# Two chains of handed-over transposes in place of one, and the near maximum between two decay multiplications, in an attention block on one core

## The reference

```python
def _L0_attn_ref(x, W_attn, W_proj):
    ...
    att = jnp.einsum('bhqd,bhkd->bhqk', q, k) * (1.0 / math.sqrt(hd))
    causal = jnp.tril(jnp.ones((T, T), dtype=bool))
    att = jnp.where(causal, att, -jnp.inf)
    att = jax.nn.softmax(att, axis=-1)
    att = att * decay_weight_matrix(T)
    y = jnp.einsum('bhqk,bhkd->bhqd', att, v)
    y = y.transpose(0, 2, 1, 3).reshape(B, T, HEAD_QKV)
    return y @ W_proj
...
h = _layernorm(x, axis=-1) * (1 + ca) + sa
x = x + ga * _L0_attn_ref(h, L0_attn_W_attn, L0_attn_W_proj)
h = _layernorm(x, axis=-1) * (1 + cb) + sb
x = x + gb * _L0_ffn_ref(h, ...)
```

## Time and profile before

| what | us |
|---|---|
| time, median of 3 runs (range) | 1622.48 (1616.28 to 1624.26) |
| the profiled execution's own time | 1620.14 |
| its span | 1618.3 |
| busy in the span: TensorE | 1301.4 |
| busy in the span: ScalarE | 1325.7 |
| busy in the span: VectorE | 974.1 |
| attention, first to last exponential | 203.4 to 1520 |

### The profile page before, as it was taken

How to read it: one execution, slowest core, us unless ns; L and a number is a source line. 1 busy time by engine, 2 the same in 40 slices (tenths; PEclk the granted TensorE clock), 3 DMA queues, 4 the chain that set the end, 5 groups by cost and what they waited for, 6 DMA issues and landing times. The chain is left out here.

```text
span 1618.3 us, 27960 instructions
## 1 busy us (share of the span) xinstructions
PE 1301.4 (80%) x11067; PEld 751.6 (46%) x11067; DVE 974.1 (60%) x1562; ACT 1325.7 (82%) x2677; POOL 52.4 (3%) x28
## 2 busy tenths in 40 slices
PE   7863188888888888888888888888888888777698
PEld 5532044444444444444444444444444444333387
DVE  5631166666666666666666666666666655544366
ACT  3433099999999999999999999999999999999532
POOL 0222000000000000000000000000000000000022
PEclk9987599999999999999999999999999999999689
DMA  4999930101010101010101010101010101000144
GB/s 165 189 232 212 147 51 1 33 2 34 1 34 1 33 1 34 1 33 2 34 1 34 1 34 1 34 1 23 9 20 11 23 9 23 8 7 1 35 152 135
DMA packets 111722, 72.95 MB, mean 45 GB/s; under 512 B 56396, under 2 KB 110947, under 8 KB 111587
## 3 DMA queue, kind: packets, MB, share of 16 engines
q1 hardware_dynamic: 111586, 71.13, 20.7%
HBM read 45.93 MB, written 25.17 MB: 44 GB/s over the span
## 5 line engine op out<-in xcount | busy, mean ns | idle before, releaser
L888 ACT ACTIVATE fast_s_ps<-fast_s_ps,fast_negmax 128x1024 f32<-128x1024 f32 (+4 forms) x768 | 789.5, 1029 | 42.4 <-PE fast_s_ps L792 40.8
L792 PE MATMUL fast_s_ps<-k_stack,fast_q_stack 96*128 96x512 bf16 (+3 forms) x2448 | 630.2, 356 | 139.4 <-ACT fast_probs L888 67.9
L918 DVE TENSOR_TENSOR fast_probsT<-fast_t_ps,fast_dec_c 128x640 f32<-128x640 f32 (+4 forms) x512 | 399.6, 780 | 216.7 <-PE fast_t_ps L812 205.7
L910 DVE TENSOR_REDUCE fast_negmax<-fast_s_ps 128x1 f32<-128x640 f32 (+4 forms) x512 | 400.1, 782 | 127.8 <-PE fast_s_ps L795 121.3
L888 ACT ACTIVATE fast_probs<-fast_s_ps,fast_negmax 128x640 f32<-128x640 f32 (+7 forms) x512 | 434.6, 849 | 51.0 <-DVE fast_negmax L910 43.7
L812 PE MATMUL fast_t_ps<-ident,fast_probs 128*128 128x128 f32 x2400 | 367.7, 282 | 102.9 <-DVE fast_yT_sb L924 50.9
L792 PEld LDWEIGHTS fast_s_ps<-k_stack,fast_q_stack 96*128 96x128 bf16 x2448 | 193.1, 98 | 400.0 <-ACT fast_probs L888 138.0
L812 PEld LDWEIGHTS fast_t_ps<-ident,fast_probs 128*128 128x128 f32 x2400 | 263.8, 141 | 201.3 <-DVE fast_yT_sb L924 85.7
L827 PE MATMUL fast_t_ps<-fast_probsT,fast_vals 128*16 128x128 f32 x4800 | 182.0, 277 | 3.9 <-DVE fast_probsT L918 2.2
L888 ACT ACTIVATION_READ_ACCUMULATOR fast_s_ps<-fast_s_ps,fast_negmax 128x1 f32 x768 | 164.2, 214 | 0.0
L827 PEld LDWEIGHTS fast_t_ps<-fast_probsT,fast_vals 128*16 128x16 f32 x4800 | 110.0, 96 | 77.1 <-issue 55.8
(11 more groups left out here) (104 smaller groups left out, 528.9 us busy)
## 6 DMA issues: line engine op xcount, KB each, us to landing
parts_d<-part SPq DMA_DIRECT2D x48, 256.0 KB, 12.4
k_stack<-parts_d SPq DMA_DIRECT2D x48, 256.0 KB, 9.6
fast_q_stack<-parts_d SPq DMA_DIRECT2D x192, 64.0 KB, 3.0
fast_vals<-v_d SPq DMA_DIRECT2D x36, 128.0 KB, 3.2
xs<-x_dram SPq DMA_DIRECT2D x8, 512.0 KB, 8.6
v_d<-w SPq DMA_DIRECT2D x8, 512.0 KB, 8.5
y_d<-fast_y_sb SPq DMA_DIRECT2D x32, 128.0 KB, 2.6
yy<-y_d SPq DMA_DIRECT2D x16, 256.0 KB, 2.7
```

The source lines that it names most:

```text
L792: last = nc.tensor.matmul(s_ps[:, n % SLOTS, o:o + w], q, k_stack[:, h, P * b0 + o:P * b0 + o + w], start=True, stop=not diag)
L888: nc.scalar.activation(dst, src, ACT.Exp, bias=negmax[:, p % 2, side, h:h + 1], scale=-1.0, accum_out=sums[:, p % 2, side, h, c:c + 1]).th ...
L910: nc.vector.tensor_reduce(out=negmax[:, p % 2, side, h:h + 1], in_=s_ps[:, n % SLOTS, max(0, cols - P * WIN):cols], axis=AX_X, op=ALU.min) ...
L918: nc.vector.tensor_tensor(probsT[:, turned(side, s), 0:nb, :], t_ps[:, 0:P * nb].rearrange("p (b q) -> p b q", q=P), dec_c[:, WIN - nb:WIN ...
```

## The change

`t_ps` gets two chains. The first bank belongs to the **head** of a unit, its first three blocks (`turn`, `decay`), and to `turn_back`. The second bank (`tail_ps`) belongs to the **tail** of a unit, its remaining one or two blocks (`turn_tail`, `decay_tail`, both new), and to the groups' values. Each chain has its own numbers and semaphores (`tail_no`, `tail_full`, `tail_free` for the second). A unit of up to three blocks has no tail.

- TensorE, near unit: the tail is turned right behind the head.
- TensorE, far unit: in a group step the head is turned ahead of part 1 of the values (before: all five blocks behind it), then come part 1, chunk 4 and only then the tail. In the other steps the tail is turned right behind the head.
- VectorE: `decay` is cut into a head and a tail. The tail of the last near unit comes behind the maximum of the near chunk of this step. The copy of a group comes between the two parts of the far unit.
- `values` waits until the tail chain is empty up to its own number, which takes in the tail of the near unit of the step before.

The diff, with the core of each place:

```diff
+            def has_tail(side, s):
+                return blocks(tile_of(s // NH, side)) > HEAD
+
+            def next_unit(side, s):
+                next_turn("unit", side, s)
+                if has_tail(side, s):
+                    next_tail("unit", side, s)
...
             for s in range(NSTEP):
                 if s > 0:
-                    next_turn("unit", NEAR, s - 1)
+                    next_unit(NEAR, s - 1)
                 if group_after(s):
-                    next_turn("group", *group_after(s))
+                    next_tail("group", *group_after(s))
                 if back_after(s):
                     next_turn("back", *back_after(s))
-                next_turn("unit", FAR, s)
+                next_unit(FAR, s)
...
+                tail_ps = t_ps[:, BANK:2 * BANK]
                 g_ps = t_ps[:, 2 * BANK - P:2 * BANK]
...
-                        for b in range(nb):
+                        for b in range(min(HEAD, nb)):
...
+                    def turn_tail(side, s):
+
+                        if not has_tail(side, s):
+                            return
+                        n = tail_no["unit", side, s]
+                        if n > 0:
+                            pe.wait_ge(tail_free, n)
...
+                        for b in range(HEAD, nb):
+                            lo = P * (b1 - b0 - nb + b)
+                            last = nc.tensor.transpose(tail_ps[:, P * (b - HEAD):P * (b - HEAD + 1)],
+                                                       probs[:, side, lo:lo + P], ident[:])
+                        last.then_inc(tail_full, 1)
+
                     def values(side, k, part):
 
-                        n = turn_no["group", side, k]
-                        pe.wait_ge(turn_free, n)
+                        pe.wait_ge(tail_free, tail_no["group", side, k])
...
                         if s > 0:
                             turn(NEAR, s - 1)
+                            turn_tail(NEAR, s - 1)
                         fill(s, 1)
                         fill(s, 2)
                         if group_after(s):
                             values(*group_after(s), 0)
                         fill(s, 3)
-                        if group_after(s):
-                            values(*group_after(s), 1)
                         if back_after(s):
                             side, done = back_after(s)
                             turn_back(done, side)
                         turn(FAR, s)
-                        fill(s, 4)
+                        if group_after(s):
+                            values(*group_after(s), 1)
+                            fill(s, 4)
+                            turn_tail(FAR, s)
+                        else:
+                            turn_tail(FAR, s)
+                            fill(s, 4)
...
-                                act.wait_ge(turn_full, turn_no["unit", side, s - 1] + 1)
+                                if has_tail(side, s - 1):
+                                    act.wait_ge(tail_full, tail_no["unit", side, s - 1] + 1)
+                                else:
+                                    act.wait_ge(turn_full, turn_no["unit", side, s - 1] + 1)
...
+                    def decay_tail(side, s):
+                        if not has_tail(side, s):
+                            return
+                        dve.wait_ge(tail_full, tail_no["unit", side, s] + 1)
+                        p, h = step_of(s)
+                        nb = blocks(tile_of(p, side))
+                        nc.vector.tensor_tensor(probsT[:, turned(side, s), HEAD:nb, :],
+                                                tail_ps[:, 0:P * (nb - HEAD)].rearrange("p (b q) -> p b q", q=P),
+                                                dec_c[:, WIN - nb + HEAD:WIN, :], ALU.mult).then_inc(tail_free, 1)
...
                         maximum(NEAR, s)
-                        if group_after(s):
-                            group_to_sb(*group_after(s))
+                        if s > 0:
+                            decay_tail(NEAR, s - 1)
...
                         decay(FAR, s)
+                        if group_after(s):
+                            group_to_sb(*group_after(s))
+                        decay_tail(FAR, s)
```

More of the change, by code:

```diff
@@ L666, in step_of, with next_tail @@
                 return s // NH, s % NH
-            turn_no = {}
+            HEAD = 3
+            turn_no, tail_no = {}, {}
             def next_turn(*job):
                 turn_no[job] = len(turn_no)
+            def next_tail(*job):
+                tail_no[job] = len(tail_no)
+            def has_tail(side, s):
[4 more added lines that the diff above has]
+                    next_tail("unit", side, s)
             def group_after(s):
@@ L688, in attention_fast @@
                 if s > 0:
-                    next_turn("unit", NEAR, s - 1)
+                    next_unit(NEAR, s - 1)
                 if group_after(s):
-                    next_turn("group", *group_after(s))
+                    next_tail("group", *group_after(s))
                 if back_after(s):
                     next_turn("back", *back_after(s))
-                next_turn("unit", FAR, s)
-            next_turn("unit", NEAR, NSTEP - 1)
+                next_unit(FAR, s)
+            next_unit(NEAR, NSTEP - 1)
             for side in (FAR, NEAR):
-                next_turn("group", side, NSTEP // HG - 1)
+                next_tail("group", side, NSTEP // HG - 1)
             for side in (FAR, NEAR):
@@ L709, in attention_fast @@
             turn_free = sem("fast_turn_free")
+            tail_full = sem("fast_tail_full")
+            tail_free = sem("fast_tail_free")
             y_stored = [sem(f"fast_y_stored{b}") for b in range(2)]
@@ L768, in _ @@
                             sp.wait_ge(s_full, PER * NH * p)
-                            sp.wait_ge(turn_full, turn_no["group", NEAR, NG4 * p - 1] + 1)
+                            sp.wait_ge(tail_full, tail_no["group", NEAR, NG4 * p - 1] + 1)
                             load(p + 1)
@@ L813, in turn @@
                         last.then_inc(turn_full, 1)
+                    def turn_tail(side, s):
[4 more added lines that the diff above has]
+                            pe.wait_ge(tail_free, n)
+                        p, _ = step_of(s)
+                        i = tile_of(p, side)
+                        b0, b1 = split(i)[0]
+                        nb = blocks(i)
+                        for b in range(HEAD, nb):
[3 more added lines that the diff above has]
+                        last.then_inc(tail_full, 1)
                     def values(side, k, part):
-                        n = turn_no["group", side, k]
-                        pe.wait_ge(turn_free, n)
+                        pe.wait_ge(tail_free, tail_no["group", side, k])
                         p, h = step_of(HG * k)
@@ L831, in values @@
                                 if b == nb - 1 and j == HG - 1:
-                                    last.then_inc(turn_full, 1)
+                                    last.then_inc(tail_full, 1)
                     def turn_back(p, side):
@@ L917, in decay @@
                         nb = blocks(tile_of(p, side))
-                        nc.vector.tensor_tensor(probsT[:, turned(side, s), 0:nb, :],
-                                                t_ps[:, 0:P * nb].rearrange("p (b q) -> p b q", q=P),
-                                                dec_c[:, WIN - nb:WIN, :], ALU.mult).then_inc(turn_free, 1)
+                        n = min(HEAD, nb)
+                        nc.vector.tensor_tensor(probsT[:, turned(side, s), 0:n, :],
+                                                t_ps[:, 0:P * n].rearrange("p (b q) -> p b q", q=P),
+                                                dec_c[:, WIN - nb:WIN - nb + n, :], ALU.mult).then_inc(turn_free, 1)
+                    def decay_tail(side, s):
[7 more added lines that the diff above has]
+                                                dec_c[:, WIN - nb + HEAD:WIN, :], ALU.mult).then_inc(tail_free, 1)
                     def group_to_sb(side, k):
-                        dve.wait_ge(turn_full, turn_no["group", side, k] + 1)
-                        nc.vector.tensor_copy(yT_sb[:, side, k % NG4, :], g_ps).then_inc(turn_free, 1)
+                        dve.wait_ge(tail_full, tail_no["group", side, k] + 1)
+                        nc.vector.tensor_copy(yT_sb[:, side, k % NG4, :], g_ps).then_inc(tail_free, 1)
                     def factors(p):
```

2 lines of the change are left out of this document (added).

## The result

The changed kernel takes 1720.97 us (median of 4 runs, 1718.82 to 1723.69), the kernel before 1622.26 us (median of 4, 1616.28 to 1624.26). The ratio is 1.0616, 95% interval 1.0584 to 1.0648. The profiled execution has a span of 1721.7 us, 103 us more than the one before.

A forecast was written before the change was run, and what follows sets the result against it. ScalarE was taken to set the pace, with group steps held by a chain through TensorE and VectorE; +0.96 us per usual group step, 83 + 6 + 5 - 6 = +88 us on 1620.1, gave 1708 us, range 1689 to 1737.

The forecast's parts named there:

- The new wait and its size: Group step: values wait for the near tail queued behind the near maximum, so part 0 starts 1.33 us later in pair 0.
- The end of the group step: From chunk 3 to the next exponential, the earlier far head shortens the chain from 3.97 to 3.60 us, gaining 0.37.
- The pairs: Sum over 126 group steps: 83 us for 86 usual ones, 6 pair 7, 5 pair 12, -6 pairs 13 to 15.
- my sum: Total of the pairs' terms, +88 us on the profiled 1620.1 us, with bounds of +69 and +117 us.
- The clock: Rival, 11%: TensorE falls to the lower clock in a quarter of 102 group steps, 33 us more, 1741 us.
- matmuls per us: Argument against the clock rival: pairs 0 to 12 would have 7.4, above pair 13 with 7.2, still at clock 1.00.
- The splits cost nothing in the plain steps: Splitting decays adds 140 ns per unit on VectorE, put at nothing in plain steps; rival, 8%: 0.14 us each, 1726 us.
- Absorbed: Rival, 5%: ScalarE's queued work covers the late values, only the end's gain counts, 47 us won, 1573 us.
- cancel: Rival, 4%: the end of a group step wins about 1.3 us, offsetting the late values, so 1620 us.

The follow-up runs named there:

- run 1: Changed kernel with VectorE's near tail decay moved ahead of the near maximum in every step: 1562.1 us, 0.9655 of the kernel before.
- run 2: Kernel before, one chain and whole decays, with only VectorE's near maximum moved ahead of the last near unit's decay: 1934.5 us in one run.
- run 4: Changed kernel with chunk 3 computed two extra times on TensorE ahead of part 0 of the values, where it waited: 1693.1 us, 1.0471 of the kernel before.
- run 5: Near tail first, plus the far tail turned behind the next step's chunk 0 and decayed behind its far maximum: 1575.4 us, 0.9755 of the kernel before.
- run 6: Changed kernel with the near tail's decay ahead of the near maximum in group steps only: 1568.0 us, 0.9696 of the kernel before.
- run 7: Early far maximum, near tail first in group steps only, and TensorE's near tail behind chunk 1 after a group step: 1551.5 us, 0.9582 of the kernel before.

## Why the prediction was right

**The new wait and its size.** Right, and within 0.03 us in pair 0. Worked out and measured, in us from the start of the group step: values 2.09 and 2.09, chunk 3 2.87 and 2.87, far head 3.31 and 3.32, copy 4.46 and 4.44, far tail 4.81 and 4.78, far maximum 5.62 and 5.60, next exponential 6.47 and 6.45. Values wait 103 times, where I had named 102; I had missed the first step of pair 13. ScalarE's waits in that step are a little shorter than forecast, 0.42 us for chunk 3 (0.5) and 0.94 for the far maximum (1.1). Outside the 21 long ones the group steps of pairs 4 to 7 take some 6.2 us, a little under the 6.3 to 6.6 that I had named. Runs 1 and 2 show that this one place in VectorE's order is the cause: moved back it turns the change into a gain, and put alone into the kernel before it costs more than the change.

**The end of the group step.** Right: a gain of 0.39 from chunk 3 on (3.97 to 3.58), 0.37 in the prediction. Run 1 has it on its own: 5.51 to 5.13.

**The pairs.** Somewhat too high. Run 4, in which the clock plays hardly a part, has a span of 1690.3 us, 72 us above the kernel before, where my sum was 88. The group steps of pairs 0 to 12 are 85 us longer in it than in the kernel before, where I had 94. In the usual group step the term was nearly right: 0.94 us in pair 0, 0.89 in pairs 4 to 6 (5.35 to 6.24), 0.77 in pair 7 (5.46 to 6.23). It was too large for the third and fifth step of each pair, which I had counted like the others: these took some 5.7 us already before and grow by only 0.59 us on average in pairs 1 to 6 and 8 to 11. For pair 12 it was too small, 0.94 us where I took 0.65. In pairs 13 to 15 the gain was too small: the group steps of these pairs sum to 126.2 us before and 117.6 after, 9 us where I took 6, and some 2.5 of the 9 are two steps that the kernel before ran at a lower clock (6.21 and 6.75 us, granted clock 0.73 and 0.71) and the changed one did not. The steps that are no group steps are 3 us shorter in run 4, where I took nothing.

**The clock.** This was a rival with 11%, for the case that a quarter of 102 group steps fall to the lower clock: 33 us. It happened in 21 of them and is worth 24 to 28 us by run 4, some 1.3 us for each, as worked out. So the time, 1721 us, is a mixture that the prediction did not name: its own mechanism at a somewhat smaller size, and most of a rival on top. That 1721 lies only 13 us above the forecast of 1708 is in part luck, since the chain came out some 16 us lower and the clock, at nothing in the sum, 24 to 28 us higher. My argument against the rival, matmuls per us averaged over pairs, did not tell: the average hides single waits of 1.25 us, and it was behind such a wait, after a stretch with TensorE busy 0.50 of 1.70 us, that the granted clock fell. The Trainium skill, TensorE: Matmul & The Clock Gate, Part 1, says that idleness lowers TensorE's clock and work restores it; the granted clock of 0.50 behind the wait and run 4 agree.

**The splits cost nothing in the plain steps.** Right: the usual one takes 4.72 us in the changed kernel, as before. There are 464 splits, not 458. VectorE is busy 1007.5 us instead of 974.1, 0.07 us per split and not 0.14. An instruction queued behind another starts some 0.08 us before that one's end, as the prediction read for the far maximum, and busy time counts such an overlap once; that would account for the difference.

**The rivals.** Absorbed and cancel did not come about; run 1 shows how little was missing for the first: the tail fits into 0.64 us of VectorE's idle time ahead of the near maximum.

## What to carry to other kernels

On an engine that works in order, look at what a short operation stands behind and at who waits for it. A tail of 0.41 us, moved behind a maximum that itself waits for TensorE, made two waits follow each other: TensorE's next instruction waited for VectorE, which had just waited for TensorE. Work that another engine waits for goes into the idle time ahead of a wait, not behind it; here the split of the chain paid only once both halves were early enough for all that count on them (runs 1 and 5). A wait on TensorE can have a second price, the clock behind it (some 28 us here), which does not show in a sum of durations. And the few steps that do something more, here the second step of a pair, are worth a look of their own: the median step does not show them (runs 6 and 7).

## What was unexpected of the hardware

Behind a wait of some 1.25 us in a step of 6 to 6.5 us the granted clock fell to 0.50 and 21 group steps took over 7 us; the other 82 of the 103 with such a wait did not. Two copies of a chunk's matmuls in its place, with no use at all, kept it at 1.00 and made the kernel 28 us faster (ratio 1.0471 against 1.0616). What picks the 21 is open.
